# VectorE turns the later groups' tokens from reloaded rows, and ScalarE copies the diagonal squares of each state update: an attention and mixture-of-experts kernel on one Trainium2 core

## Chip, cores and metric

The kernel runs on one core of a Trainium2 chip (trn2), in one launch. The metric is the device time in microseconds (us). The engines are TensorE (PE), VectorE (DVE), ScalarE (ACT), GpSimd (POOL) and SyncE (SP), which issues most DMAs; they work side by side, each through its own instructions in order, and wait for one another on semaphores.

## What is computed

The input x has 4 x 1024 tokens of 512 features. Each token is normalised over its features (xn). Then comes chunked linear attention with 16 heads of 32 features and chunks of 128 tokens, cut here to what matters:

```python
q, k, v = silu(xn @ Wq), silu(xn @ Wk), silu(xn @ Wv)      # 16 heads of 32
for each chunk of 128 tokens:                             # S: 32 x 32 per head, starts at 0
    o = ((q k^T) * D) v + (q S) * q_decay
    S = chunk_decay * S + (k * k_decay)^T v
gate = (xn @ Wg1) @ Wg2
y = (rmsnorm per head of (o * sigmoid(gate))) @ Wo         # added to x
```

The second part is a mixture of 8 experts (512 to 2048 to 512, ReLU) over the same xn: each token goes to its two best experts by the logits xn @ Wg, an expert takes at most 1280, and the results, weighted by a softmax, are added to the output. The residual x is added too. All of it is float32; PE's products are made of three products of rounded high parts and remaining low parts (hi*hi, hi*lo, lo*hi).

## The kernel before

There are 32 tiles of 128 tokens. Attention works on groups of four tiles (512 tokens; `g` = 0 to 7, half a sequence each), and in each group on four units (`i` = 0 to 3, four heads each), 32 units `u` in all. After them come the experts, in which PE is busy without a gap; the change touches none of their code, except that some tensors lie elsewhere.

**Normalised tokens.** For each tile VectorE takes mean and variance (`norm_pair`, L971), GpSimd the power -0.5 (`norm_scale`, L549), VectorE writes `xn` (`normalise`, L982, the instruction L986). SP stores xn to DRAM (`store_xn`, L424), from where the experts gather it later. PE turns the tile with four 128x128 transposes into a PSUM bank (`turn_xn`, L1421, which calls `turn`, L1388, the instruction L1390). ScalarE copies the bank rounded to `xnT_hi` (`xnT_high`, L753), VectorE makes `xnT_lo`, the bank less the high part (`xnT_low`, L989). For group g + 1 this happens in unit i = 2 of group g, behind the last q projection of group g; tiles 2 and 3 of group g + 1 are normalised at the end of unit i = 1 of group g, tiles 0 and 1 at the end of the unit i = 3 before it (in group 0, all four in unit 0).

**Order on PE in a unit u** (L1580 to L1632): scores of u (`score`, L1427), state update of u (`update_states`, L1474, unless it was made ahead, as for i = 2 from group 1 on), gate of u (`project_gate`, L1470), k and q projections of u + 1 (`project`, L1396; 12 products of 128x512 each, listed under `product`, L1383), in unit i = 2 the transposes of xn, in unit i = 3 the small projection (L1407), then the transposes of the decayed k of u + 1 (`turn_kd`, L1465), attention of u (`attend`, L1489: products with the states L1502, with the masked scores L1508). In unit i = 1 the output projection of the group before follows (`project_out`, L1512), in unit i = 3 the v projection of the next group.

**Order on ScalarE in a unit** (L853 to L878): tanh of the gate, squares of the unit before, silu of k and of q of u + 1, in unit i = 2 the four high parts, then the copy of the turned k (`copy_kd`, L847), the high part of the attention output (`oT_high`, L804).

**Order on VectorE in a unit** (L1213 to L1273): the states, the masks on the four score banks (`mask`, L1014), the mean squares, scaling and turning back of earlier units, in unit i = 2 the four low parts, the gating (`gate_output`, L1091), a block transpose (`turn_gated`, L1096), in unit i = 1 residuals and the normalisation of two tiles.

**The state update.** PE writes kd^T v of each head into the diagonal 32x32 square of its chunk's 128x128 block in `t_bank`; the rest of the block holds old values. `states` (L1071) multiplies the bank by `same_head`, a 0/1 mask, into `update`, and then makes three steps of decay:

```python
step(v_.tensor_tensor(update[:, 0:n, :], by_chunk(t_bank[:, :])[:, 0:n, :],
                      same_head[:, :].unsqueeze(1).to_broadcast([P, n, P]), ALU.mult))
```

`n` is 4 in even groups and 3 in odd ones.

**SP's queue** is written out by hand (L448 to L526). At the start: the decays, four tiles of x, the four parts each of Wq and Wk, Wg1 and the router's Wg (one DMA each, into `small_raw`), Wg2 four times, the norm's weights, four stores of xn, then Wv and Wo (which wait for staging buffers), four more tiles of x. ScalarE reads `small_raw` behind the high parts of Wk, and the high parts of Wv after that.

## Time and profile before

| | us |
|---|---|
| median of 3 runs | 1984.32 (1983.89 to 1984.41) |
| the profiled execution | 1986.43 |
| its span, first to last instruction | 1984.7 |
| PE busy | 1972.2 (99%) |
| DVE busy | 906.7 (46%) |
| ACT busy | 552.5 (28%) |
| POOL busy | 730.1 (37%) |

The granted TensorE clock is 1.00 over the whole span (2.4 GHz). Shares of busy time are means over both parts of the kernel; the attention lies before some 535 us. Matmuls are pipelined: one of 128x512 shows as 0.39 us and the next starts 0.23 us after it, so a step's cost on PE is read from the starts of successive instructions. Times in a timeline are us from the start of the span; "x16" is the number of instructions merged in a row, and the brackets hold the idle time of the engine before it, with what ended it.

### The profile page before, as it was taken

What the parts mean: (1) busy time and instruction counts of PE and PEld (TensorE: products, weight loads), DVE (VectorE), ACT (ScalarE), POOL (GpSimd) and SP (SyncE); (2) the same over time, 40 slices, a digit from 0 to 9 for tenths busy, and PEclk for the clock granted to TensorE, in tenths of its full rate; (3) what the DMA queues carried; (4) which work ended last, traced back from release to release, by engine and by line L of the source; (5) the groups of instructions that cost most, each with busy time, mean ns of one, the idle gap of its engine ahead of it and who ended that gap; (6) DMA issues with size and microseconds to landing.
All of it is one profiled execution on the core that took longest, in us unless ns stands there. A gap on an engine that the chain in (4) does not pass through costs nothing.

```text
span 1984.7 us, 28995 instructions
## 1 busy us (share of the span) xinstructions
PE 1972.2 (99%) x11672; PEld 1631.0 (82%) x11672; DVE 906.7 (46%) x1839; ACT 552.5 (28%) x994; POOL 730.1 (37%) x608
## 2 busy tenths in 40 slices
PE   9999999999999999999999999999999999999998
PEld 7888888888888888888888888888888888888887
DVE  8777676777753234224323422432343234334311
ACT  6322232223332123124212312321242123123211
POOL 4645454545343324313342431333143324233321
PEclk9999999999999999999999999999999999999999
DMA  6112122211452134315233421522162125224121
GB/s 206 67 66 87 43 68 68 84 63 48 131 153 39 47 75 125 42 55 126 66 67 74 126 42 56 125 65 42 47 159 45 43 51 157 37 62 102 42 33 22
DMA packets 85638, 151.50 MB, mean 76 GB/s; under 512 B 18432, under 2 KB 18432, under 8 KB 85488
## 3 DMA queue, kind: packets, MB, share of 16 engines
q1 hardware_dynamic: 61312, 105.64, 16.8%
q0 software_dynamic: 24176, 43.76, 13.0%
q8 instruction: 106, 1.74, 0.4%
q14 instruction: 44, 0.36, 0.1%
HBM read 109.82 MB, written 39.53 MB: 75 GB/s over the span
## 4 chain that ended last, share of the span: by engine, by line
PE 97%; DVE 1%; SPq 1%; DMA 0%; issue 0%; POOL 0%; ACT 0%; DVEq 0%
PE bank L1383 47%; PE bank L1687 35%; PE bank L1519 5%; PE bank L1437 2%; PE bank L1508 2%; PE bank L1390 1%; PE bank L1502 1%; PE bank L1743 1%; PE bank L1730 1%; PE bank L1472 1%; PE bank L1411 1%; PE bank L1482 1%; DMA attn_raw<-in_L_attn_Wv 0%; PE bank L1531 0%; SPq L446 0%
## 5 line engine op out<-in xcount | busy, mean ns | idle before, releaser
L1303 DVE SCALAR_TENSOR_TENSOR h_lo<-bank,h_hi 128x512 fp32r<-128x512 f32 x254 | 175.3, 690 | 722.9 <-ACT h_hi L904 683.7
L682 POOL DMA_INDIRECT gathered<-xn_rows,gather_row x304 | 315.5, 1038 | 483.6 <-DVE x_blocks L1153 316.8
L1383 PE MATMUL bank<-xT_lo,w_hi 128*128 128x512 f32 x1024 | 398.5, 389 | 0.5 <-issue 0.5
L1383 PE MATMUL bank<-xT_hi,w_hi 128*128 128x512 f32 x1024 | 398.7, 389 | 0.0
L1383 PE MATMUL bank<-xT_hi,w_lo 128*128 128x512 f32 x1024 | 398.4, 389 | 0.0
L1687 PE MATMUL bank<-w_hi,h_hi 128*128 128x512 f32 x1016 | 395.2, 389 | 0.0
L1687 PE MATMUL bank<-w_lo,h_hi 128*128 128x512 f32 x1016 | 395.2, 389 | 0.0
L1687 PE MATMUL bank<-w_hi,h_lo 128*128 128x512 f32 x1016 | 395.2, 389 | 0.0
L904 ACT ACTIVATE h_hi<-bank 128x512 fp32r<-128x512 f32 x254 | 151.7, 597 | 795.5 <-PE bank L1383 756.3
L703 POOL DMA_INDIRECT out_rows<-y,add_row x64 | 103.9, 1624 | 435.7 <-ACT y L897 419.6
L1383 PEld LDWEIGHTS bank<-xT_lo,w_hi 128*128 128x128 f32 x1024 | 192.2, 188 | 40.9 <-issue 1.0
L1383 PEld LDWEIGHTS bank<-xT_hi,w_hi 128*128 128x128 f32 x1024 | 192.2, 188 | 40.8 <-issue 0.7
L1383 PEld LDWEIGHTS bank<-xT_hi,w_lo 128*128 128x128 f32 x1024 | 192.2, 188 | 39.9
L1687 PEld LDWEIGHTS bank<-w_lo,h_hi 128*128 128x128 f32 x1016 | 190.7, 188 | 39.8
L1687 PEld LDWEIGHTS bank<-w_hi,h_lo 128*128 128x128 f32 x1016 | 190.7, 188 | 39.6
L1687 PEld LDWEIGHTS bank<-w_hi,h_hi 128*128 128x128 f32 x1016 | 190.7, 188 | 39.4
L1123 DVE TENSOR_TENSOR w_lo<-raw_weights,w_hi 128x512 fp32r<-128x512 f32 x256 | 167.8, 684 | 84.8 <-ACT w_hi L802 64.9
L802 ACT CAST w_hi<-raw_weights 128x512 fp32r<-128x512 f32 x256 | 150.0, 618 | 98.3 <-DMA raw_weights<-in_L_ffn_w 78.8
L636 POOL TENSOR_TENSOR head_scale<-mean_sq,minus_half 128x16 f32<-128x16 f32 x32 | 104.4, 3264 | 20.7 <-DVE mean_sq L1025 20.2
L628 POOL DMA_INDIRECT slot_table<-record,slot_no x64 | 65.5, 1024 | 103.7 <-DVE slot_no L1069 47.4
L1018 DVE TENSOR_TENSOR scores<-bank,intra_decay 128x512 f32<-128x512 f32 x128 | 79.2, 681 | 0.4 <-PE bank L1437 0.3
L1163 DVE TENSOR_TENSOR xT_lo<-x_blocks,xT_hi 128x512 fp32r<-128x512 f32 x68 | 48.4, 711 | 52.3 <-ACT xT_hi L845 52.3
(225 smaller groups left out, 2298.5 us busy)
## 6 DMA issues: line engine op xcount, KB each, us to landing
raw_weights<-in_L_ffn_w SPq DMA_DIRECT2D x256, 256.0 KB
x_in<-in_L_attn_x SPq DMA_DIRECT2D x32, 256.0 KB, 4.0
xn_rows<-xn SPq DMA_DIRECT2D x32, 256.0 KB
x_res<-in_L_attn_x SPq DMA_DIRECT2D x32, 256.0 KB, 4.9
out_rows<-y_attn SPq DMA_DIRECT2D x28, 256.0 KB
gathered<-xn_rows,gather_row POOLq DMA_INDIRECT x304
out_rows<-y,add_row POOLq DMA_INDIRECT x88, 5.8
attn_raw<-in_L_attn_Wq SPq DMA_DIRECT2D x4, 256.0 KB, 4.7
```

The lines of the kernel that those rows point to most:

```text
L628: pool.indirect_dma_start(table[:, :], bass.IndirectOffsetOnAxis(ap=slot_no[:, t, i:i + 1], axis=0), record[:, t, i, :], None, bounds_chec ...
L636: g_.tensor_tensor(head_scale[:, u % 2, :], mean_sq[:, u % 2, :], minus_half[:, :], ALU.pow).then_inc(S["head_scale_ready"], 1)
L682: pool.indirect_dma_start(xg[:, nth % 2, q * P:(q + 1) * P], None, xn_pieces, bass.IndirectOffsetOnAxis(ap=gather_row[:, col, q:q + 1], ax ...
L703: pool.indirect_dma_start(out[:, :], bass.IndirectOffsetOnAxis(ap=add_row[:, col:col + 1], axis=0), y[:, i, :], None, compute_op=ALU.add). ...
L802: a.copy(unit_parts(u)[0], raw[:, u % UNITS, :]).then_inc(S["ffn_hi"], 1)
L904: a.activation(h_parts(e, j, f)[0][:, 0:n * P], h_bank[f % 2][:, 0:n * P], ACT.Relu).then_inc(S["h_hi_ready"], 1)
L1018: v_.tensor_tensor(by_chunk(scores[:, r, :]), by_chunk(sc[r][:, :]), decay_cols(intra_decay[:, u % GROUPS * HPG + r, :]), ALU.mult).then_i ...
L1123: v_.tensor_tensor(lo, raw[:, u % UNITS, :], hi.bitcast(F32), ALU.subtract).then_inc(S["ffn_lo"], 1)
L1303: v_.scalar_tensor_tensor(lo[:, 0:n * P], h_bank[f % 2][:, 0:n * P], 0.0, hi[:, 0:n * P].bitcast(F32), ALU.max, ALU.subtract).then_inc(S[" ...
L1383: last = mm(dest, at(left[l], t), at_r(right[r], t), start=(i == 0), stop=(i == n - 1))
L1519: last = mm(bank[:, :], oT[l][:, t, part], (w_hi["o"], w_lo["o"])[r][:, t, :], start=(start and t == ks[0] and l == r == 0), stop=(stop an ...
L1687: last = mm(y_bank[i][:, :], hx[:, part], wx[c][:, f % FPC, :], start=(f == 0 and l == 0), stop=(f == FT - 1 and l == 2))
```

## The change

1. The transposes of xn on PE fall away for groups 1 to 7. After its store, SP loads each tile of xn back from DRAM (`reload_pieces`), in four DMAs of 32 tokens each, 64 KB, 512 bytes per partition: 32-partition block q holds feature quarter q. VectorE turns the tile by one STREAM_TRANSPOSE of 128x512, which turns each 32x32 block by itself (`turn_pieces`): tiles 0 and 1 in unit i = 1, tiles 2 and 3 in unit i = 2. The high and low parts then read these blocks in SBUF. The result lies in the place of the tile before (`xn_blocks`), so `normalise` waits for low parts instead of transposes.
2. Features come into the k-tiles in another order, so the rows of Wq, Wk, Wv, Wg1 and the router's Wg are loaded in that order (`by_quad`), Wg1 and the router's Wg in four DMAs each instead of one. The first group's tiles are turned on PE by `turn_by_quads`, 16 products with 32 output partitions per tile.
3. In unit i = 3 PE's k projection takes the products by parts (`project_next_k`): hi*hi and lo*hi wait for the high parts, hi*lo for the low parts. The waits for low parts before the scores and the gate of that unit fall away. ScalarE's `copy_kd` stands between high parts 1 and 2.
4. ScalarE copies the four diagonal squares of the update (`copy_update`, four instructions of 32 partitions) into `update`, which is zeroed once; the multiplication and `same_head` fall away.
5. On VectorE the normalisation of tiles 2 and 3 moves ahead of residuals 2 and 3; SP's queue follows.

```diff
+            def reload_pieces(t):
+                j = t % TPG
+                sp.wait_ge(xn_stored[j], 16 * (t // TPG + 1))
+                for i in range(QUADS):
+                    first = t * P + i * HD
+                    sp.dma_start(xn[:, j, i * P:(i + 1) * P], xn_dram[first:first + HD, :].rearrange("s (q f) -> q s f", q=QUADS)
+                                 ).then_inc(xn_pieces_loaded[j], 16)
...
-            sp.dma_start(small_raw[:, :, 0:HD], wg1.rearrange("(t p) n -> p t n", p=P)).then_inc(S["small_loaded"], 16)
-            sp.dma_start(small_raw[:, :, HD:], w_route.rearrange("(t p) n -> p t n", p=P)).then_inc(S["small_loaded"], 16)
+            for t in range(DT):
+                sp.dma_start(small_raw[:, t, 0:HD], by_quad(wg1)[t]).then_inc(S["small_loaded"], 16)
+                sp.dma_start(small_raw[:, t, HD:], by_quad(w_route)[t]).then_inc(S["small_loaded"], 16)
...
                 if u == 0:
                     for t in range(TPG, 2 * TPG):
                         store_xn(t)
+                    for t in range(TPG, 2 * TPG):
+                        reload_pieces(t)
...
                 if i == 1 and g > 0:
-                    for j in range(TPG):
-                        store_y(TPG * (g - 1) + j)
+                    store_y(TPG * (g - 1))
+                    store_y(TPG * (g - 1) + 1)
                     if g < SUPERS - 1:
                         store_xn(TPG * (g + 1) + 2)
                         store_xn(TPG * (g + 1) + 3)
+                    store_y(TPG * (g - 1) + 2)
+                    if g < SUPERS - 1:
+                        reload_pieces(TPG * (g + 1) + 2)
+                        reload_pieces(TPG * (g + 1) + 3)
+                    store_y(TPG * (g - 1) + 3)
...
                     if g < SUPERS - 3:
                         load_x(TPG * (g + 3))
                         load_x(TPG * (g + 3) + 1)
+                    if g < SUPERS - 2:
+                        reload_pieces(TPG * (g + 2))
+                        reload_pieces(TPG * (g + 2) + 1)
...
+            def copy_update(u):
+                act.wait_ge(S["updated"], u + 1)
+                act.wait_ge(S["update_zeroed"], 1)
+                wait(act, ("attended", u))
+                n = carried_chunks(u)
+                for r in range(HPG):
+                    rows = slice(r * HD, (r + 1) * HD)
+                    last = a.copy(update[rows, 0:n, rows], by_chunk(t_bank[:, :])[rows, 0:n, rows])
+                last.then_inc(S["update_copied"], 1)
...
             for u in range(ATTN_UNITS):
                 g, i = u // GROUPS, u % GROUPS
+                copy_update(u)
                 act.wait_ge(S["gate_projected"], u + 1)
...
                 if i == 2 and g < SUPERS - 1:
                     for j in range(TPG):
+                        if j == 2:
+                            copy_kd(u + 1)
                         xnT_high(TPG * (g + 1) + j)
...
+            def turn_pieces(t):
+                j = t % TPG
+                dve.wait_ge(xn_pieces_loaded[j], 16 * QUADS * (t // TPG))
+                wait(dve, ("xn_turned", t))
+                v_.transpose(xn_blocks(j), xn[:, j, :]).then_inc(S["xn_turned"], 1)
...
-                dve.wait_ge(S["updated"], u + 1)
+                dve.wait_ge(S["update_copied"], u + 1)
                 dve.wait_ge(S["decay_made"], 1)
-                dve.wait_ge(S["consts_made"], 12)
-                step(v_.tensor_tensor(update[:, 0:n, :], by_chunk(t_bank[:, :])[:, 0:n, :],
-                                      same_head[:, :].unsqueeze(1).to_broadcast([P, n, P]), ALU.mult))
...
                 if i == 2 and g < SUPERS - 1:
+                    turn_pieces(TPG * (g + 1) + 2)
+                    turn_pieces(TPG * (g + 1) + 3)
                     for j in range(TPG):
                         xnT_low(TPG * (g + 1) + j)
...
+                if i == 1 and g < SUPERS - 1:
+                    turn_pieces(TPG * (g + 1))
+                    turn_pieces(TPG * (g + 1) + 1)
...
+            def turn_by_quads(bank, rows_of_tile):
+                for t in range(DT):
+                    for q in range(QUADS):
+                        rows, first = slice(q * HD, (q + 1) * HD), q * P + t * HD
+                        last = mm(bank[rows, t * P:(t + 1) * P], rows_of_tile[:, first:first + HD], ident[:, :], start=True, stop=True)
+                return last
...
+            def project_next_k(g):
+                pe.wait_ge(S["xnT_hi_made"], TPG * (g + 1))
+                for nth, (w_part, x_part, t) in enumerate(hi_hi + lo_hi + hi_lo):
+                    if nth == 2 * DT:
+                        pe.wait_ge(S["xnT_lo_made"], TPG * (g + 1))
+                    last = mm(proj[1][:, :], w_part["k"][:, t, 0:P], x_part[:, t, :], start=(nth == 0), stop=(nth == 3 * DT - 1))
+                last.then_inc(S["k_projected"], 1)
...
-                if i == 2 and g < SUPERS - 1:
-                    pe.wait_ge(S["masked"], HPG * (u + 1))
-                    turn_xn(g + 1, lambda j: pe.wait_ge(S["k_ready" if j == 2 else "q_ready"], u + 2) if j > 1 else None)
```

## Rows read from the trace of the kernel before

**Rows 1.** The page's chain of work that ended last, share by engine.
```profile
PE 97%; DVE 1%; SPq 1%; DMA 0%; issue 0%; POOL 0%; ACT 0%; DVEq 0%
```
**Rows 2.** PE's waits: line, released by, us in total, times, longest.
```profile
PE bank L1508 <- DVE scores L1018: 1.0, 1, 1.0
```
**Rows 3.** Timeline of PE at a group's turn: start us, us, what.
```profile
317.42 1.91 PE L1390 MATMUL bank<-ident,xn 128*128 128x128 f32 x16
319.16 0.60 PE L1390 MATMUL bank<-ident,kdT 128*128 128x128 f32 x4
...
322.48 0.46 PE L1482 MATMUL bank<-v,kd 128*32 128x32 f32 x32
...
323.20 0.39 PE L1383 MATMUL bank<-xnT_hi,wk_hi 128*128 128x512 f32 x1
323.43 0.40 PE L1383 MATMUL bank<-xnT_lo,wk_hi 128*128 128x512 f32 x1
```
**Rows 4.** Timeline of SP's queue in the start.
```profile
6.94 0.47 SPq L453 DMA_DIRECT2D small_raw<-in_L_attn_Wg  x1
7.46 0.54 SPq L454 DMA_DIRECT2D small_raw<-in_L_ffn_Wg  x1
...
12.84 2.78 SPq L446 DMA_DIRECT2D attn_raw<-in_L_attn_Wv  x4
```
**Rows 5.** Chain that ended last, the start: start us, us, what.
```profile
17.40 0.64 ACT wv_hi L767
...
37.89 1.44 DVE state L1083
...
42.15 1.08 PE bank L1508 x32
```
**Rows 6.** Timeline of VectorE, units i = 1 and i = 2 of a group.
```profile
302.46 0.69 DVE L1118 TENSOR_TENSOR y_attn<-bank,x_res 128x512 f32<-128x512 f32 x1 [1.70 <-PE bank L1519]
...
305.18 0.69 DVE L1118 TENSOR_TENSOR y_attn<-bank,x_res 128x512 f32<-128x512 f32 x1 [0.35 <-PE bank L1519]
...
311.23 0.99 DVE L986 TENSOR_SCALAR xn<-x_in,moments,rstd 128x512 f32<-128x512 f32 x2
312.13 0.68 DVE L1079 TENSOR_TENSOR update<-bank,same_head 128x512 f32<-128x512 f32 x1
...
317.80 0.71 DVE L1108 STREAM_TRANSPOSE normed<-squares 128x512 f32<-128x512 f32 x1
```
**Rows 7.** Issue to landing: x_in's 32 loads; slot_rec's eight, median.
```profile
DMA to landing us min/median/max: 3.1/4.0/6.5
...
slot_rec<-slot_table SPq DMA_DIRECT2D x8, 40.0 KB, 1.8
```
**Rows 8.** Timeline of PE: three tiles turned in quarters.
```profile
518.85 2.83 PE L1531 MATMUL bank<-ident,y 128*32 128x128 f32 x96
```
**Rows 9.** Timeline of ScalarE at the same turn as rows 3.
```profile
317.62 0.60 ACT L772 ACTIVATE qT<-bank 128x512 f32<-128x512 f32 x1 [2.12 <-PE bank L1383]
318.11 2.05 ACT L757 CAST xnT_hi<-bank 128x512 fp32r<-128x512 f32 x4
```
**Rows 10.** Groups by shape (busy us, mean ns); x_blocks' instructions (ns min/median/max).
```profile
L850 ACT COPY kd<-bank 128x384 f32<-128x384 f32 x16 | 7.8, 487 | 0.1
...
L845 ACT CAST xT_hi<-x_blocks x68: 619/622/625, 577.3 to 1887.5; 128x512 fp32r<-128x512 f32 x68
L1163 DVE TENSOR_TENSOR xT_lo<-x_blocks,xT_hi x68: 691/710/733, 578.0 to 1888.3; 128x512 fp32r<-128x512 f32 x68
```
**Rows 11.** Timelines of GpSimd and of VectorE, 317 to 355 us.
```profile
317.25 3.31 POOL L636 TENSOR_TENSOR head_scale<-mean_sq,minus_half 128x16 f32<-128x16 f32 x1 [0.39 <-DVE mean_sq L1025]
321.65 1.28 POOL L589 TENSOR_TENSOR qdT<-qT,q_decay 128x512 f32<-128x512 f32 x1 [1.09 <-PE bank L1508]
...
351.43 3.31 POOL L636 TENSOR_TENSOR head_scale<-mean_sq,minus_half 128x16 f32<-128x16 f32 x1 [0.80 <-DVE mean_sq L1025]
...
353.38 0.69 DVE L1112 TENSOR_TENSOR oT_lo<-normed,oT_hi 128x512 fp32r<-128x512 f32 x1 [0.68 <-ACT oT_hi L808]
```

More of the change, by code:

```diff
@@ L255, in build @@
         x_res_loaded = [sem(f"x_res_loaded{i}") for i in range(TPG)]
+        xn_pieces_loaded = [sem(f"xn_pieces_loaded{i}") for i in range(TPG)]
         xn_stored = [sem(f"xn_stored{i}") for i in range(TPG)]
@@ L380, in squares_of, with xn_blocks @@
             return squares[:, u % 2, :]
+        def xn_blocks(j):
+            return xn_first_blocks[:, :] if j == 0 else xn[:, j - 1, :]
         def turned_xn(t):
-            bank = (first_xn_bank if t < TPG else xn_bank)[t % TPG]
-            return bank[:, :].rearrange("p (t c) -> p t c", t=DT)
+            if t < TPG:
+                return first_xn_bank[t][:, :].rearrange("p (t q c) -> p t q c", t=DT, q=QUADS)
+            return xn_blocks(t % TPG).rearrange("p (q t c) -> p t q c", q=QUADS, t=DT)
         def small_bank(g):
@@ L415, in by_k_tile, with by_quad @@
             return blocks[:, :].rearrange("p (q t c) -> p t q c", q=QUADS, t=DT)
+        def by_quad(w):
+            return w.rearrange("(q t d) n -> t q d n", q=QUADS, t=DT)
         @block.sync
@@ L445, in load_weights @@
                 w = (wq, wk, wv, wo)[u // DT]
-                sp.dma_start(attn_raw[:, u % UNITS, :], w[u % DT * P:(u % DT + 1) * P, :]).then_inc(attn_raw_loaded[u % UNITS], 16)
+                rows = w[u % DT * P:(u % DT + 1) * P, :] if u // DT == WSET.index("o") else by_quad(w)[u % DT]
+                sp.dma_start(attn_raw[:, u % UNITS, :], rows).then_inc(attn_raw_loaded[u % UNITS], 16)
             sp.dma_start(ld_row[:, :], log_decay.partition_broadcast(P)).then_inc(S["decays_loaded"], 16)
@@ L755, in xnT_high @@
                 act.wait_ge(S["xn_turned"], t + 1)
-                wait(act, ("k_projected", GROUPS * (t // TPG)))
-                a.copy(xnT_hi[:, :, j * P:(j + 1) * P], turned_xn(t)).then_inc(S["xnT_hi_made"], 1)
+                wait(act, ("k_projected", GROUPS * (t // TPG)), ("q_projected", GROUPS * (t // TPG)))
+                a.copy(token_cols(xnT_hi, j), turned_xn(t)).then_inc(S["xnT_hi_made"], 1)
             def weights_high(n, ts=range(DT)):
@@ L864, in _ @@
                     for j in range(TPG):
+                        if j == 2:
+                            copy_kd(u + 1)
                         xnT_high(TPG * (g + 1) + j)
-                if i == GROUPS - 1 and g < SUPERS - 1:
-                    copy_logits(g + 1)
-                if u < ATTN_UNITS - 1:
+                elif u < ATTN_UNITS - 1:
+                    if i == GROUPS - 1:
+                        copy_logits(g + 1)
                     copy_kd(u + 1)
@@ L984, in normalise @@
                 dve.wait_ge(S["rstd_ready"], t // 2 + 1)
-                wait(dve, (xn_stored[j], 16 * (t // TPG)), ("xn_turned", t - TPG + 1))
+                in_use = ("xn_turned", t - TPG + 1) if t < 2 * TPG else ("xnT_lo_made", t - TPG + 1 + (j < TPG - 1))
+                wait(dve, (xn_stored[j], 16 * (t // TPG)), in_use)
                 v_.tensor_scalar(xn[:, j, :], x_in[:, j, :], moments[:, j, 0:1], rstd[:, j:j + 1],
@@ L990, in xnT_low @@
                 j = t % TPG
-                cols = slice(j * P, (j + 1) * P)
                 dve.wait_ge(S["xnT_hi_made"], t + 1)
-                v_.tensor_tensor(xnT_lo[:, :, cols], turned_xn(t), xnT_hi[:, :, cols].bitcast(F32), ALU.subtract).then_inc(S["xnT_lo_made"], 1)
+                v_.tensor_tensor(token_cols(xnT_lo, j), turned_xn(t), token_cols(xnT_hi, j).bitcast(F32),
+                                 ALU.subtract).then_inc(S["xnT_lo_made"], 1)
+            def turn_pieces(t):
[3 more added lines that the diff above has]
+                v_.transpose(xn_blocks(j), xn[:, j, :]).then_inc(S["xn_turned"], 1)
             def weights_low(n, ts=range(DT)):
@@ L1167, in _ @@
             v_.tensor_scalar(diff[:, :], diff[:, :], 0.0, None, ALU.max).then_inc(S["diff_ready"], 1)
+            v_.memset(update[:, :, :], 0.0).then_inc(S["update_zeroed"], 1)
             v_.memset(taken[:, :], 0.0).then_inc(S["carry_zero"], 1)
@@ L1257, in _ @@
                         normalise(TPG * (g + 1) + 3)
-                    else:
+                    add_residual(TPG * (g - 1) + 2, proj[0])
+                    add_residual(TPG * (g - 1) + 3, proj[1])
+                    if g == SUPERS - 1:
                         first_used = spares_of(dve, 0)
@@ L1430, in score @@
                 wait(pe, ("masked", HPG * u))
-                if u % GROUPS == GROUPS - 1 and u < ATTN_UNITS - 1:
-                    pe.wait_ge(S["xnT_lo_made"], TPG * (u // GROUPS + 1) + 2)
                 for c in range(TPG):
@@ L1527, in turn_first @@
                 pe.wait_ge(S["masked"], HPG * (ATTN_UNITS - 1) + sc.index(first_bank[i]) + 1)
-                for t in range(DT):
-                    for q in range(QUADS):
-                        rows, first = slice(q * HD, (q + 1) * HD), q * P + t * HD
-                        last = mm(first_bank[i][rows, t * P:(t + 1) * P], y[:, i, first:first + HD], ident[:, :], start=True, stop=True)
-                last.then_inc(S["x_turned"], 1)
+                turn_by_quads(first_bank[i], y[:, i, :]).then_inc(S["x_turned"], 1)
             pe.wait_ge(S["consts_made"], 6)
@@ L1540, in _ @@
             keep_clock(40)
[L1541 removed]
+            turn_first_xn()
             keep_clock(8)
```

41 lines of the change are left out of this document (16 added, 25 removed).

## The prediction

> **What bounds the kernel now.** I read the chain of waits first: TensorE (PE) holds 97% of the span [rows 1]. PE's own waits come next: after the start-up they come to 1.0 us for VectorE's masks, at the first attention product, and nothing else worth naming [rows 2]. So an instruction taken from PE after the start is worth its whole pitch, and any wait put in front of PE costs its whole length. Two places decide: the start (to 43 us), which hangs on DMA issues and VectorE, and the turn from one group of four tiles to the next, seven times.
>
> **Part 1: the transposes of xn leave PE.** In each of seven groups PE turns four tiles with 16 transposes, starting at 317.42 us; the next instruction, kd's transpose, starts at 319.16 [rows 3]. The pitch, not the 1.91 us busy, is the price: 1.74 us. 7 x 1.74 = **-12.2 us**. The four tiles of the first group stay on PE.
>
> **Part 2: the start.** SP issues serially, 0.47 and 0.54 us for the two small loads, and Wv's loads begin at 12.84 [rows 4]. The change makes these two loads eight: 8 x 0.47 - 1.0 = +2.75 us for all behind them. Wv's issue is on the chain: 4.56 us to its use by ScalarE at 17.40, from there VectorE's splits, routing and states, to the mask that PE awaits until 42.15 [rows 5]. ScalarE waits for the last small load in the same queue, so it shifts by the same 2.75. On VectorE the mask of unit 0 comes 2.75 later, less the 0.68 of the removed multiplication [rows 6]: +2.05. PE's own work after its count of choices, pushed by the same 2.75, reaches that product at 42.15 - 1.0 + 2.75 = 43.9, +1.75. The later one holds: **+2.0 us**. Bounds: if Wv lands in the shortest 3.1 us of [rows 7], 1.4 comes back, +0.6. If the eight reordered loads of Wq and Wk and the eight small ones all cost 0.54 instead of 0.47, it is 1.1 more, +3.1. One state update of this chain took 1.44 us [rows 5], long for its size; that may shrink (PE's own +1.75 then holds).
>
> PE turns the first tiles in quarters now. Three such tiles took 2.83 us [rows 8], 0.94 each against 0.44 by transposes. That is +2.0 us before 13 us, beside the queue's delay: the small loads and Wv come later still, so it costs nothing. Were the queue not late, it would be the bound, with some +1. The memset of `update` lies in VectorE's wait for its first load, and the two dropped affine selects free only GpSimd: nothing.
>
> **Part 3: the turn of the group, without the 1.74 us.** I take the group at 311 us as model, in its old times. PE's last q product ends where the transposes began, 317.42. The rest follows 1.74 earlier: the update starts at 320.74 instead of 322.48, the next k projection at 321.46 instead of 323.20 [rows 3]. That projection wants all four high parts at 321.46, all low parts after eight products of 0.23, at 323.3, and the q projection wants the tanh after twelve, at 324.2.
>
> ScalarE: silu q starts at 317.62, then high parts at a pitch of 0.51 [rows 9]. Read from SBUF such a cast takes 0.62 us [rows 10] instead of 0.61: nothing. Parts 0 and 1 end by 319.2, kd is copied by 319.8 (wanted at 320.7), parts 2 and 3 end by 320.9: **0.6 us to spare**.
>
> VectorE: residual 1 starts at 305.18; the two normalisations (0.99) move from 311.23 to behind it, into a wait for PE, and the multiplication (0.68) goes from 312.13. So turning back, which ended at 318.5, ends near 316.9 [rows 6]. Two block transposes of 0.71 (the same instruction and shape [rows 6]) end near 318.3. Each low part takes at most 0.71 [rows 10] and follows its high part; the last ends near 321.6 (wanted 323.3), the gating near 322.3. Tiles 0 and 1 are turned a unit earlier, 1.4 us for both in a 1.70 us wait for PE [rows 6]. Without that cover they would delay the first residual, after which PE still has a whole product row to do. Cost on the path: zero.
>
> ScalarE's copy of the diagonal squares is four instructions of 32x128. The nearest row is the 128x384 copy of 0.49 us [rows 10]; I take 0.25 each by length, 1.0 in all. Bounds: nothing, and 4 x 0.49 = 2.0. Behind PE's update, at 321.2, it ends at 322.2, so the tanh can run from 322.3 (the gating) to 322.9, with 1.3 us to spare; with 2.0 it still ends at 323.8, 0.4 to spare. Queued behind it are tanh, square and silu k. VectorE's states wait for the copy instead of multiplying, -0.68 + 1.0; PE waits for masks nowhere after the start [rows 2]. Zero.
>
> SP: per group 16 issues more, some 7 us of its time. The tight ones are tiles 2 and 3. Normalised by 306.9, stored from 306.5, a store lands after about 4.0 us, the median of x's loads of 256 KB [rows 7]. Eight issues of 0.47 follow, from 310.5 to 314.3; the last 64 KB land between 1.8 us (40 KB) and 4.0 us after their issue at 313.8 [rows 7]: 316 to 318. The last piece may land at 320.2 without a cost to PE (0.7 for the turn and 0.6 for the high part before 321.46). The store of y and the loads of x and residuals queued behind these issues are wanted tens of us later. Zero.
>
> **Sum.** -12.2 + 2.0 = -10.2. The profiled execution took 1986.43 us (span 1984.7 and 1.7 around it): it would give 1976.2. The runs' median is 1984.32, 2.1 lower: **1974.1 us**. Own range of this case: 0.6 to 3.1 at the start, 1972.7 to 1975.2.
>
> **A port against it.** What I see: VectorE's oT_lo, two SBUF inputs, started at 353.38 and took 0.69 us while GpSimd's head scaling ran from 351.43 to 354.74; the same scaling stands at 317.25 to 320.56 here [rows 11]. So I let the low parts run beside it, though they are new in having both inputs in SBUF (one was PSUM). The Trainium skill (SBUF — State Buffer, "Who interferes with whom") says that a VectorE operation with two SBUF inputs and a GpSimd one that reads SBUF exclude each other for the full instruction. By that rule the sum would be near zero (rival D); rows 11 speak against it for this scaling.
>
> **Rivals.**
> B, the start is cheap: what the issues delay had slack. Against: Wv's loads are in the chain itself. -12.2 with at most 0.6 back: 1972.1 to 1972.7.
> C, small waits: the 0.6 us of the high parts or the tanh's time are eaten by slower SBUF reads or GpSimd's decayed q (1.28 us [rows 11]) beside the low parts. For: three engines hand over in 4 us; against: each step above has its margin. 0.2 to 1.0 us x 7: 1975.5 to 1981.
> D, the port: low part 0 waits for 320.56, decayed q gets in between (1.3), low parts end at 324.4, the gating at 325.1, the tanh at 325.7 against 324.2: 1.5 x 7 = 10.5, 1984.6.
> E, slower than before: the reload comes late. Place: turning tile 3 of each group. With 6.5 us, the longest landing of [rows 7], for store and reload, and 0.54 per issue, the last piece lands at 306.5 + 6.5 + 7 x 0.54 + 6.5 = 323.3 instead of 320.2: 3.1 x 7 = 22, 1996. It decides the sign from 1.46 us per group (10.2 / 7), a landing after 321.7. Against: 6.5 is the longest of 32.
> F, PE spends the time otherwise (a lower granted clock or longer pitches): 1984. PE stays busy, so little for it.
>
> **Chances.** Forecast 0.56, B 0.10, C 0.21, D 0.05, E 0.06, F 0.02. A measurement tells 0.2% (4 us) from no change: faster is below 1980.4. Forecast, B and nearly all of C lie there: 0.85; same 0.08 (rest of C, D, F); slower 0.07 (E, a late D). The range takes B, the forecast and C, 1971.5 to 1980.5.
>
> **What would show it.** Right: PE has no transposes of xn after the start; kd's transpose follows the last q product at once in each third unit; the first attention product stands near 44.2 instead of 42.15; Wv is issued near 15.6. Wrong: PE idle ahead of the k projection released by ScalarE's xnT_hi (a late reload if VectorE waits for a DMA first; C otherwise), by VectorE's xnT_lo (D), or ahead of q by the tanh; or a first attention product at 42 to 43 us (B).

## The result and the profile after

The changed kernel is slower: 2012.62 us median of 4 runs (2010.08 to 2013.88) against 1984.16 us (1983.89 to 1984.41) for the kernel before on the same chip, a ratio of 1.0142 (95% interval 1.0127 to 1.0157). The forecast was 1974.1 (range 1971.5 to 1980.5) and faster. The profiled execution took 2011.84 us, its span is 2010.0. The profiled execution of the kernel before (1986.43) lies 2.3 us above its median, so the traces differ by 25.3 us where the runs differ by 28.5; where the 2.3 us lie is said further down.

**Where the time went.** Three starts of PE's products cut the attention into pieces. Timeline of PE of the changed kernel, at the first attention product and at the first product of the first and of the seventh output projection (columns as in [rows 3]):

```profile
74.91 1.08 PE L1562 MATMUL bank<-scores,v 128*32 128x128 f32 x32
...
138.81 0.50 PE L1573 MATMUL bank<-wo_hi,oT_hi 128*128 128x512 f32 x1
...
517.05 0.50 PE L1573 MATMUL bank<-wo_hi,oT_hi 128*128 128x512 f32 x1
```

The same two output projections of the kernel before:

```profile
106.13 0.50 PE L1519 MATMUL bank<-wo_hi,oT_hi 128*128 128x512 f32 x1
...
494.52 0.50 PE L1519 MATMUL bank<-wo_hi,oT_hi 128*128 128x512 f32 x1
```

| us | before | after | after less before |
|---|---|---|---|
| start to the first attention product | 42.15 | 74.91 | +32.8 |
| from there to the first output projection (holds the first turn of a group) | 63.98 | 63.90 | -0.1 |
| six more groups (six turns) | 388.39 | 378.24 | -10.2 |
| the rest, experts above all (span less the above) | 1490.2 | 1493.0 | +2.8 |
| span | 1984.7 | 2010.0 | +25.3 |

The turns of the groups pay (though 2.3 of the 10.2 us are not the change's doing, see under the table of experiments), and the start takes over three times as much back. PE's waits of the changed kernel say what the start waited for (columns as in [rows 2]):

```profile
PE bank L1432 <- DVE wv_lo L1051: 11.3, 4, 4.4
PE bank L1600 <- ACT xnT_hi L782: 5.8, 1, 5.8
PE bank L1600 <- ACT wk_hi L792: 3.8, 2, 1.9
PE bank L1588 <- POOL ident L578: 2.7, 1, 2.7
PE bank L1432 <- issue: 2.3, 1, 2.3
PE bank L1432 <- DVE g1T_parts L1059: 0.5, 1, 0.5
PE bank L1573 <- ACT tanh_g L894: 0.3, 1, 0.3
```

The first three, 20.9 us, are new but for 0.3 us, and all are high or low parts of loaded weights or of tokens queued behind them. The mask's wait of [rows 2] is gone. ScalarE's timeline shows the loads behind it, one 256 KB load per 2.67 us:

```profile
9.58 0.63 ACT L792 ACTIVATE wq_hi<-attn_raw 128x512 fp32r<-128x512 f32 x1 [2.42 <-DMA attn_raw<-in_L_attn_Wq]
12.25 0.63 ACT L792 ACTIVATE wq_hi<-attn_raw 128x512 fp32r<-128x512 f32 x1 [2.04 <-DMA attn_raw<-in_L_attn_Wq]
...
22.94 0.63 ACT L792 ACTIVATE wk_hi<-attn_raw 128x512 fp32r<-128x512 f32 x1 [2.04 <-DMA attn_raw<-in_L_attn_Wk]
```

And SP's queue, which answers to [rows 4]:

```profile
3.13 2.45 SPq L467 DMA_DIRECT2D attn_raw<-in_L_attn_Wq  x4
5.62 11.03 SPq L467 DMA_DIRECT2D attn_raw<-in_L_attn_Wk  x4
16.69 2.55 SPq L475 DMA_DIRECT2D small_raw<-in_L_attn_Wg  x1
...
34.17 3.33 SPq L467 DMA_DIRECT2D attn_raw<-in_L_attn_Wv  x4
```

Wq's four issues still take 0.6 us each. Wk's four and the first three small ones take about as long as a load, 2.55 to 3.2 us: SP stands in its queue, which I read as full. The small loads wait there, and Wv is issued at 34.17 instead of 12.84 [rows 4]. The table of windows says how much moved (first a window, then busy us and number of instructions of each engine, granted PE clock, share of the 16 DMA engines, GB/s); after:

```profile
10.00:20.00 10.00, 4.46 (x136) 4.02 (x124) 2.27 (x5) 3.88 (x8) 1.18 (x7) 0.91 0.27 100
20.00:30.00 10.00, 5.95 (x12) 3.57 (x13) 4.30 (x8) 2.67 (x5) 0.00 (x0) 0.50 0.25 80
```

and before, 10 to 20 us:

```profile
10.00:20.00 10.00, 9.71 (x51) 7.79 (x51) 9.92 (x18) 9.43 (x24) 1.53 (x10) 1.00 1.09 358
```

With everything waiting for weights, the DMA engines were a quarter busy. That is as much as 4 of 16 at full work, each moving its part at its usual rate (358 / 16 is 22 GB/s, 100 / 4 is 25). PE, left idle, then ran its few products at a granted clock of 0.50, the 1.2 GHz level.

### The profile page after: what moved, and what is told of

The parts are those of the page before. It is cut to its first block, busy times and chain, and to the rows that moved or that the text cites. A ratio compares the mean times of both kernels' runs of the same rounds, so it can differ in the third digit from the quotient of the medians.

```text
span 2010.0 us, 29268 instructions
## 1 busy us (share of the span) xinstructions
PE 1976.5 (98%) x11672; PEld 1625.5 (81%) x11672; DVE 920.1 (46%) x1836; ACT 584.6 (29%) x1122; POOL 732.4 (36%) x606
## 4 chain that ended last, share of the span: by engine, by line
PE 94%; SPq 2%; DMA 2%; DVE 1%; issue 1%; ACT 0%; POOL 0%; DVEq 0%; ACTq 0%
PE bank L1432 46%; PE bank L1745 35%; PE bank L1573 4%; PE bank L1491 1%; PE bank L1562 1%; PE bank L1801 1%; PE bank L1788 1%; PE bank L1556 1%; DMA attn_raw<-in_L_attn_Wv 1%; PE bank L1439 1%; SPq L467 1%; DMA xn<-xn_rows 1%; PE bank L1460 1%; PE bank L1615 1%; PE bank L1526 1%
## 5 line engine op out<-in xcount | busy, mean ns | idle before, releaser
L1166 DVE TENSOR_TENSOR w_lo<-raw_weights,w_hi 128x512 fp32r<-128x512 f32 x256 | 167.7, 685 | 83.5 <-ACT w_hi L827 83.2
```

The lines of the kernel that those rows point to most:

```text
L1166: v_.tensor_tensor(lo, raw[:, u % UNITS, :], hi.bitcast(F32), ALU.subtract).then_inc(S["ffn_lo"], 1)
```

## The experiments

The medians of the kernel before on the chips used lie between 1984.16 and 1987.62 us, so a time counts only beside the kernel before of its own chip. "Start" is the time of the first attention product, "groups" the six intervals between output projections.

| kernel | us (before there) | ratio, 95% | start | groups |
|---|---|---|---|---|
| before | 1984.16 | | 42.15 | 388.39 |
| after | 2012.62 (1984.16) | 1.0142, 1.0127 to 1.0157 | 74.91 | 378.24 |
| b_split4 | 1986.67 (1986.68) | one run | 42.45 | 388.44 |
| b_small8 | 1989.37 (1986.68) | one run | 45.87 | 388.40 |
| a_stride4 | 1984.21 (1986.68) | one run | 46.33 | 380.57 |
| a_all | 1978.87 (1986.68) | 0.9960, 0.9946 to 0.9975 | 43.68 | 378.25 |
| a_q32 | 1987.72 (1984.36) | one run | 51.39 | 379.26 |
| b_dims | 2008.63 (1984.36) | one run | 66.07 | 386.14 |
| a_quarter | 2009.14 (1984.36) | one run | 75.46 | 376.11 |
| a_all48 | 1974.24 (1984.36) | 0.9949, 0.9933 to 0.9966 | 43.26 | 376.12 |
| a_all40 | 1977.69 (1984.43) | 0.9963, 0.9952 to 0.9975 | 43.22 | 376.15 |
| b_keep48 | 1990.37 (1984.43) | 1.0030, 1.0019 to 1.0042 | 43.69 | 386.14 |
| a_mult | 1982.22 (1984.43) | 0.9988, 0.9978 to 0.9997 | 44.71 | 381.91 |
| b_copy | 1983.07 (1984.43) | 0.9995, 0.9985 to 1.0005 | 40.93 | 386.14 |
| b_quad | 2014.84 (1987.62) | 1.0136, 1.0119 to 1.0153 | 69.52 | 388.48 |
| a_keep48 | 2011.21 (1987.62) | 1.0119, 1.0102 to 1.0136 | 73.71 | 381.76 |

In seven traces (before, b_split4, b_small8, a_stride4, a_all, b_quad, a_keep48) the seventh output projection comes late, by 2.1 to 2.4 us where a like group is there to compare, behind stops of PE without a releaser. a_all shows them, and the identical a_all40 on another chip does not. The six of them that are experiments are all those of two chips, on which the kernel before has its two highest medians (1986.68 and 1987.62); none of the eight traces of the two other chips (medians 1984.36 and 1984.43) shows them. So this much of a "groups" figure goes with the chip or the hour and not with the kernel.

### Is it the pattern of the weight loads?

**b_split4**, the kernel before with the rows of its loads split 4 x 32, though they follow one another in memory:

```diff
-sp.dma_start(attn_raw[:, u % UNITS, :], w[u % DT * P:(u % DT + 1) * P, :])
+rows = w[u % DT * P:(u % DT + 1) * P, :].rearrange("(q d) n -> q d n", q=QUADS)
+sp.dma_start(attn_raw[:, u % UNITS, :], rows)
```

> The kernel before, where the loads of Wq, Wk and Wv keep their natural rows and only their access pattern is written as 4 x 32 rows instead of 128. Theory S (spread: a load whose DRAM pattern begins with a dimension of 4 is served by 4 of the core's 16 DMA engines, so that 256 KB take the 2.67 us seen between the changed kernel's high parts of Wq, and the queue behind them stands): the same 2.67 us between Wq's high parts, the DMA share near 0.26 in that stretch, the first attention product (L1508, at 42.15 in the kernel before) at 58 to 68 us, the whole at 2000 to 2010. Rival R (rows scattered in DRAM make the reordered loads slow): nothing changes, 42 us and 1984. Rival N (the number of small loads, 8 instead of 2, does it): also 42 us and 1984.

Nothing changed (start 42.45). Such a split describes the same unbroken run of rows, so it tests nothing about scattered ones. A test needs a pattern whose pieces don't follow one another.

**b_small8**, the kernel before with its two small loads as eight, of consecutive rows:

```diff
-sp.dma_start(small_raw[:, :, 0:HD], wg1.rearrange("(t p) n -> p t n", p=P))
-sp.dma_start(small_raw[:, :, HD:], w_route.rearrange("(t p) n -> p t n", p=P))
+for t in range(DT):
+    sp.dma_start(small_raw[:, t, 0:HD], wg1[t * P:(t + 1) * P, :])
+    sp.dma_start(small_raw[:, t, HD:], w_route[t * P:(t + 1) * P, :])
```

> The kernel before, where only the two small loads (Wg1 and the router's Wg) are made as eight, each of 128 natural rows. My prediction's term: Wv's issue 2.75 us later, the first attention product at 44.2 us instead of 42.15 and the whole +2.0 us, 1986. Theory S says the same, since each of these loads begins with 128 rows. Rival N (the count of small loads is what costs the changed kernel its start): first attention product beyond 60 us, 2004 or more.

The start came 3.4 us after b_split4's and the run took 2.7 us more (one run of each). This is the part of the start that the prediction had priced (+2.0, bounds 0.6 to 3.1), somewhat above it.

**a_stride4**, the changed kernel with every fourth feature in one k-tile: a load then takes every fourth row, one per partition, and its pattern begins with 128. VectorE writes xn in the matching order.

```diff
-return w.rearrange("(q t d) n -> t q d n", q=QUADS, t=DT)
+return w.rearrange("(p t) n -> t p n", t=DT)
...
-v_.tensor_scalar(xn[:, j, :], x_in[:, j, :], moments
+v_.tensor_scalar(xn[:, j, :].rearrange("p (q t f) -> p q f t", q=QUADS, t=DT),
+                 x_in[:, j, :].rearrange("p (q f t) -> p q f t", q=QUADS, t=DT), moments
```

> The changed kernel with another order of features: xn is written with every fourth feature of a quarter together, so that k-tile t holds rows t, t+4, t+8 ... of each weight, and each load of Wq, Wk, Wv (and of the experts' first matrix) has one dimension of 128 rows with a stride of four rows. The eight small loads stay eight. Theory S: high parts of Wq follow each other at ScalarE's own pace (0.67 us), first attention product at 44 to 45 us instead of 75.0, the whole at 1976 to 1979 (before - 12.2 + 2.0 + 2 for waits at the groups' turns). Rival R (scattered rows): the rows are more scattered than in the changed kernel, so 75 us and 2010 stay.

28.6 of the 32.8 us were back, with rows that are scattered more than the change's. The forecast was missed all the same: a start of 46.33 where 44 to 45 was expected, and 1984.21 us where 1976 to 1979 was. Of the excess, some 2 us are the stops before the seventh projection and 2.4 another stop (further down). The edit also gives the experts' first matrix this order. That is not what brings the time back: behind the seventh output projection, a_keep48 with the old pattern takes 1489.5 us and a_all48 with the new one 1489.1. **a_all** adds to it two small loads instead of eight and the reload of a_quarter (below):

> As the kernel with every fourth feature together, and besides: the small loads are two again, and the four reloads of a tile go by quarters of features (32 partitions x 4 x 512 bytes, first dimension 32) instead of by 32 tokens (first dimension 4). Theory S: each reload is spread over 16 DMA engines, tile 3 no longer makes VectorE wait at the group's turn, first attention product at 42 to 43 us, the whole 1971 to 1974, about 0.6% below the kernel before. If the waits at the turn come from GpSimd beside the low parts instead (rival D of the prediction, in small), they stay, and it is 1973 to 1976.

It gained, though less than forecast (1978.87 for 1971 to 1974, start 43.68 for 42 to 43). Its remaining loss led to the questions further down.

**a_q32** keeps every row of the changed kernel in its slot and turns only the loads round: one takes the 128 rows of a feature quarter, 32 partitions by 4 slots.

```diff
-sp.dma_start(attn_raw[:, u % UNITS, :], by_quad(w)[u % DT])
+sp.dma_start(attn_raw[q * HD:(q + 1) * HD, base:base + DT, :],
+             w[q * P:(q + 1) * P, :].rearrange("(t d) n -> d t n", t=DT))
```

> The changed kernel with the same weight rows in the same slots, fetched the other way round: one load takes the 128 features of a quarter (32 partitions, 4 slots each, so the pattern begins with 32) instead of 4 quarters of one slot (the pattern begins with 4); the gating and routing weights likewise. Bytes, addresses, order and number of loads are the same. Theory S (a load whose pattern begins with a dimension of 4 runs on 4 of the 16 DMA engines): Wk's last load lands by 28 us, Wv is issued by 18 us, the first attention product comes at 44 to 48 us and the span is 1979 to 1985 us. Rival R (2 KB rows from scattered places are slow by themselves): the loads still come one per 2.7 us, first attention product at 70 to 76, span about 2010.

23.5 us came back and rival R fell: the same rows in as many loads don't come one per 2.7 us. But the start missed its forecast of 44 to 48, and Wv was issued at 19.42, not by 18. Two things in the trace may be why; they were not priced apart: the first high part now needs all four loads of its weight (it starts at 12.36, in the changed kernel at 9.58), and the DMA engines were fully busy yet moved 210 GB/s, where the kernel before moved 358. Window of a_q32:

```profile
10.00:20.00 10.00, 7.86 (x146) 5.90 (x141) 6.04 (x11) 6.31 (x12) 1.17 (x7) 1.00 1.12 210
```

**b_dims** makes a scale of it: the kernel before with the first dimension 2 for Wq, 8 for Wk, 16 for Wv.

```diff
+n = (2, 8, 16, 1)[u // DT]
+rows = w.rearrange("(q t d) n -> t q d n", q=n, t=DT)[u % DT]
```

> The kernel before, with the rows of Wq, Wk and Wv taken in other orders, so that their loads begin with a dimension of 2, 8 and 16 (it leaves the order of the features against the tokens wrong, so attention's values differ; the work is the same). Theory S (16 engines divided by the first dimension): Wq's four loads come one per 5.3 us, Wk's one per 1.3 us, Wv's at the full rate, 0.7 us or less each. Rival R (scattered rows are slow whatever the pattern's first dimension): Wq, Wk and Wv come at one and the same spacing, near 2.7 us. Rival W (each load's reordering is free, the queue's depth was the trouble): all under 1 us.

Timeline of ScalarE, where Wq (2) and Wk (8) arrive:

```profile
11.84 0.63 ACT L769 ACTIVATE wq_hi<-attn_raw 128x512 fp32r<-128x512 f32 x1 [4.73 <-DMA attn_raw<-in_L_attn_Wq]
17.19 0.63 ACT L769 ACTIVATE wq_hi<-attn_raw 128x512 fp32r<-128x512 f32 x1 [4.72 <-DMA attn_raw<-in_L_attn_Wq]
...
33.01 0.63 ACT L769 ACTIVATE wk_hi<-attn_raw 128x512 fp32r<-128x512 f32 x1 [0.59 <-DMA attn_raw<-in_L_attn_Wk]
34.35 0.63 ACT L769 ACTIVATE wk_hi<-attn_raw 128x512 fp32r<-128x512 f32 x1 [0.71 <-DMA attn_raw<-in_L_attn_Wk]
```

and its window from 15 to 20 us, when only Wq's loads ran:

```profile
15.00:20.00 5.00, 0.00 (x0) 0.00 (x0) 0.00 (x0) 0.63 (x1) 0.00 (x0) 0.50 0.14 50
```

5.35 us per load with 2, 2.67 with 4, 1.34 with 8: inverse to the first dimension, at 0.14 and 0.26 of the engines for 2 and 4. The figure for 8 is one pair of starts. Wv's spacing (16) is hidden by other waits and was not read off.

**b_quad** puts the change's own pattern, alone, into the kernel before.

```diff
+rows = w.rearrange("(q t d) n -> t q d n", q=QUADS, t=DT)[u % DT]
```

> The kernel before with one thing of the change: Wq, Wk and Wv are loaded by the changed kernel's pattern, one row block of each of the 4 quarters (it leaves the order of the features against the tokens wrong, so attention's values differ; the work is the same). Theory S: the pattern that begins with 4 costs the start by itself: one Wq or Wk load per 2.67 us, first attention product at 70 to 74 us instead of 42, time 28 to 33 us above the kernel before, 2012 to 2017. Rival: most of the changed kernel's loss needs its eight small loads or its turns by quarter as well, and this alone costs under 20 us.

Start 69.52, ratio 1.0136 against the change's 1.0142. So the pattern of Wq, Wk and Wv by itself is 27.4 of the 32.8 us. The start ended just under the expected band; the time is inside 2012 to 2017, but only 27.2 us above the kernel before of its chip, for 28 to 33. The other 5.4 us of the start come with what the changed kernel adds. In its trace eight small loads stand in the slow queue (Wv issued at 34.17 there, 29.49 here); this part was not tested by itself.

The Trainium skill ("DMA: Bandwidth & Descriptors", "How many engines (k)") states the rule: the number of engines is the largest up to 16 that divides the slowest dimension of both patterns. The runs agree at 2, 4 and 8. By that rule alone the eight loads of Wq and Wk would have been priced at four times their time. So they would by the trace of the kernel before, as the last part shows.

### What a turn of a group is worth

**a_quarter**, the changed kernel with its reload turned round: 32 source rows per partition block come first, instead of the 4 feature quarters.

```diff
-sp.dma_start(xn[:, j, i * P:(i + 1) * P], xn_dram[first:first + HD, :].rearrange("s (q f) -> q s f", q=QUADS))
+sp.dma_start(by_chunk(xn[i * HD:(i + 1) * HD, j, :]),
+             xn_dram[t * P:(t + 1) * P, i * P:(i + 1) * P].rearrange("(c s) f -> s c f", c=QUADS))
```

> The changed kernel, the reload of the normalised rows alone turned round (32 rows of each of the 4 row blocks, pattern beginning with 32, instead of 32 rows by 4 stretches of 512 bytes, also beginning with 32 in the source). Theory: the start is untouched (first attention product 74 to 76), the turning of tile 3 waits less for its reload than the 0.7 us of the changed kernel, span 2008 to 2011. Rival: the reload matters more than its waits show, and the span falls under 2006.

(The text on record says that the changed kernel's reload also begins with 32. It doesn't, it begins with 4 and is the same fault in small.) VectorE's waits of the changed kernel had this line:

```profile
DVE xn L1040 <- DMA xn<-xn_rows: 6.9, 6, 1.6
```

In a_quarter it is gone and the six groups take 376.11 instead of 378.24 us. While the pieces of tile 3 are under way (401 to 404 us in both traces) the DMA share is 0.25 in the changed kernel and 0.48 in a_quarter. So 0.35 us a group was rival E in small: VectorE turned tile 3 late and passed it on. In the changed kernel, VectorE at a turn:

```profile
410.06 0.71 DVE L1040 STREAM_TRANSPOSE xn<-xn 128x512 f32<-128x512 f32 x1 [0.69 <-DMA xn<-xn_rows]
410.70 0.65 DVE L1032 TENSOR_TENSOR xnT_lo<-xn_first_blocks,xnT_hi 128x512 fp32r<-128x512 f32 x1
411.27 2.97 DVE L1032 TENSOR_TENSOR xnT_lo<-xn,xnT_hi 128x512 fp32r<-128x512 f32 x3
414.16 0.67 DVE L1137 SCALAR_TENSOR_TENSOR gated<-tanh_g,bank 128x512 f32<-128x512 f32 x1
```

and GpSimd beside it:

```profile
407.44 3.39 POOL L661 TENSOR_TENSOR head_scale<-mean_sq,minus_half 128x16 f32<-128x16 f32 x1
410.92 1.57 POOL L614 TENSOR_TENSOR qdT<-qT,q_decay 128x512 f32<-128x512 f32 x1
```

**b_copy**, the kernel before with the second half of the change alone (ScalarE's four copies, no multiplication):

> The kernel before with that half alone: ScalarE copies the diagonal squares, VectorE no longer multiplies, TensorE still turns the tokens. Theory: neither engine bounds the units here, so the time stays that of the kernel before within 1.5 us. Rival: the copies (0.96 us before each unit's tanh) delay the gate, TensorE waits for it in each unit, and the time rises by 0.2 to 0.5 us a unit, 6 to 15 us in all; or, the other way, the states come earlier and the kernel gains 1.5 to 4 us.

Within 0.1% of the kernel before. The groups keep their old pace, 64.56 and 64.15 us in turn. The start is 1.2 us earlier and PE's wait for the mask is gone. **a_mult**, the reverse: a_all48 (below) with the multiplication back on VectorE.

```diff
-copy_update(u)
...
+step(v_.tensor_tensor(update[:, 0:n, :], by_chunk(t_bank[:, :])[:, 0:n, :],
+                      same_head[:, :].unsqueeze(1).to_broadcast([P, n, P]), ALU.mult))
```

> a_all48 with VectorE's multiplication by the same-head table in place of ScalarE's four copies (both tables built as in the kernel before). It prices the second half of the change. Theory P (the copies are what keeps VectorE in time at the turn of a group): VectorE carries 0.62 us more in each of 31 units, the low parts of the turned tokens come later, TensorE waits at the turn, and the time is 2 to 6 us above a_all48's, 1976 to 1980. Rival Q (VectorE has room; the copies only move work): within 1 us of a_all48's 1974.2 (ratio to before 0.994 to 0.9955).

Theory P held, and more than expected: 8 us above a_all48, for 2 to 6. 5.8 of them are in the groups, 1.5 in the start and 1.5 between the start and the first output projection; the experts were 0.4 faster. PE's waits name VectorE, at another place than expected, the gate's low part of the next group:

```profile
PE bank L1442 <- DVE g1T_parts L1065: 4.0, 7, 0.9
```

The two halves belong together: the copies alone bring nothing that the runs can tell, and without them most of what the turns save goes back into VectorE's waits.

### A stop of PE that comes and goes with eight instructions far ahead of it

The changed kernel has a stop that the kernel before doesn't have, in the third expert, with no releaser. In the program it stands two products behind the branch over the code of the spare blocks, which lies in the middle of each expert. Timeline of PE, after:

```profile
1009.08 0.39 PE L1432 MATMUL bank<-xT_lo,w_hi 128*128 128x512 f32 x1
1011.75 0.80 PE L1432 MATMUL bank<-xT_hi,w_lo 128*128 128x512 f32 x1 [2.28 <-issue]
1012.34 0.63 PE L1432 MATMUL bank<-xT_hi,w_hi 128*128 128x512 f32 x1
1012.77 0.63 PE L1432 MATMUL bank<-xT_lo,w_hi 128*128 128x512 f32 x1
```

It stands in front of the same product in a_stride4, a_all, a_q32 and a_quarter (2.28 to 2.51 us). Here and in a_all PE comes back at the lower clock: the next products follow at 0.43 us instead of 0.23. The kernel before has 0.54 us at the like place of its seventh expert (the texts on record say the eighth, and count the two halves of an expert as experts of their own in places):

```profile
1718.86 0.50 PE L1383 MATMUL bank<-xT_lo,w_hi 128*128 128x512 f32 x1 [0.54 <-issue]
```

**a_all48** is a_all with eight transposes more at the start, where PE waits for x anyway:

```diff
-keep_clock(40)
+keep_clock(48)
```

> a_all with 48 instead of 40 transposes that keep TensorE's clock up at the start, while it waits for x; nothing else in the program is other, but TensorE's later instructions lie 8 places further on. Theory I (the 2.5 us stop two products into an expert, without a releaser, is TensorE running out of fetched instructions at one place of its code): the stop goes or moves to another product; if it goes, the time falls by 3 to 4.5 us to 1974.5 to 1976. Rival J (the stop belongs to the work, its data or its timing): it stays at the second product of an expert with 2.3 to 2.5 us and the time is a_all's 1978.9.

> a_all once more (40 transposes at the start), to stand beside its pair with 48 on one chip's kernel before. Theory I (TensorE's stop of 2.5 us belongs to the place of its code): the stop is there again at the third product of the same expert, and the ratio to the kernel before is 0.9965 to 0.998, 2 to 3 thousandths above that with 48 (0.9949). Theory J (the stop comes and goes by chance): no stop, and a ratio near 0.995.

> The kernel before with 48 instead of 40 transposes at the start, while TensorE waits for x. The kernel before has a stop of 0.54 us without a releaser at the second product of its eighth expert. Theory I: eight instructions more move the places of the code, so this stop changes its size or its expert, and the time moves by up to 3 us either way while the work up to there keeps its times. Theory J: the stop stays at 0.2 to 0.8 us in the eighth expert and the time is that of the kernel before within 1 us.

> The changed kernel with 48 transposes at the start instead of 40. Theory I (TensorE's stop of 2.28 us in the third expert belongs to the place of its code): as in the pair of a_all, the stop is gone, and the time falls 2 to 4 us to 2008.5 to 2010.5; ratio to before 1.012 to 1.013. Rival J: the stop stays.

The stop did what theory I said in all four; the sizes were at or beyond the edge of what was expected (a_all48 1974.24 for 1974.5 to 1976, a_all40 0.9963 for 0.9965 to 0.998, a_keep48 2011.21 for 2008.5 to 2010.5, b_keep48 5.9 us for up to 3). With 48, a_all and the changed kernel lose the stop altogether, and a_mult, with 48 too, has none; a_all40, on a third chip, has it again at the same product (2.21 us). The pair gives 0.9949 against 0.9963, of which the intervals overlap, so the size of the gain, some 2 to 3 us, rests on the traces. The changed kernel with 48 has a ratio of 1.0119 against 1.0142, again with overlapping intervals. In the kernel before the same eight instructions do the opposite. A stop of 1.56 us appears in the second expert and that in the seventh grows from 0.54 to this, with the low clock behind it:

```profile
1720.51 0.80 PE L1383 MATMUL bank<-xT_hi,w_lo 128*128 128x512 f32 x1 [2.45 <-issue]
1721.11 0.63 PE L1383 MATMUL bank<-xT_hi,w_hi 128*128 128x512 f32 x1
1721.53 0.63 PE L1383 MATMUL bank<-xT_lo,w_hi 128*128 128x512 f32 x1
```

It is 6 us slower for it, interval clear of 1. All six traces of the changed kernel's family with 40 have the large stop in the third expert, although they reach it at times from 978 to 1012 us, and none of the three with 48 has. That speaks for the place of PE's code and against its timing, but no run moved the code without adding instructions, and the mechanism was not tried. The small stop of the kernel before has another size in each trace (0.16 us in b_small8, 0.82 in b_split4) though PE's code is the same there.

## Why the prediction was wrong

**What bounds the kernel, right.** PE was the bound, and a wait put in front of it cost its whole length: PE's three new waits make up 20.9 of the 32.8 us of the start. The rest was not divided further; the lower clock between 20 and 60 us (granted 0.50, 0.74, 0.60 and 0.55 in steps of 10 us) is a part of it.

**Part 1, right in size, one turn short.** In six groups the change saved 10.2 us against 6 x 1.74 = 10.4. That near match is luck, of two things that cancel: 2.3 us of the old 388.39 are the stops that go with the chip, and 2.1 us was lost to the late reload. Cleaned of both, a group went from 64.36 us (half of 64.57 + 64.14) to 62.66 (a_quarter, a_all48, half of 62.83 + 62.49): 1.70 against 1.74. The seventh turn, the one in group 0, gave 0.1 instead of 1.74, also in a_all48 (63.90). There VectorE still carries work of the start. In a_all48 PE's k projection at 65 to 68 us runs 0.6 us long and the gate's low part costs 0.5 more at 79 us.

**Part 2, the step that failed.** "SP issues serially, 0.47 and 0.54 us": the eight reordered loads of Wq and Wk, and Wv's, were priced by their issues alone, with at most 1.1 us for a slightly longer issue. The term that was missing is the transfer. A load whose pattern begins with the 4 quarters runs on a quarter of the DMA engines, 2.67 us instead of about 0.7. Wq and Wk are then 21 us of transfer, and once some of them are under way each issue behind them takes as long. The diff's `rearrange("(q t d) n -> t q d n")` was where to see it, and its price stood in the trace of the kernel before, which loads the experts' first matrix by that very pattern (`unit_source`, L372). SP's timeline there, and the window in which four such loads of 256 KB run almost alone (columns as in the windows above):

```profile
448.06 7.54 SPq L468 DMA_DIRECT2D raw_weights<-in_L_ffn_w  x8
...
508.76 2.47 SPq L468 DMA_DIRECT2D raw_weights<-in_L_ffn_w  x4
```

```profile
512.00:522.00 10.00, 9.90 (x211) 8.32 (x210) 8.77 (x18) 6.05 (x12) 6.47 (x3) 1.00 0.28 101
```

That is 101 GB/s, 2.6 us a load, against 358 GB/s in the start (window of 10 to 20 us above). Even the slow issue is there: of the eight in a row from 448.06 the sixth took 2.64 us. In the experts ScalarE waits for such loads (83.5 us in all) and PE doesn't, so they cost nothing; in the start PE waits too. The small loads' own term, +2.0, measured 3.4 by itself. "The longest landing" of rival E looked at the reload with the same blind spot; it cost 0.35 us a group, where the rival had 3.1.

**The turns by quarters, right.** They cost nothing while the queue was late. Where the queue is not (a_all48) the start is 43.26, with PE busy throughout from 10 us: the "+1" that the prediction gave for this case.

**Part 3, right, with thinner margins.** ScalarE's copies took 0.95 to 1.07 us for four (1.0 forecast). The block transposes took 0.67 to 0.71. The low parts did not take "at most 0.71" each: at every turn one of the later three took 1.67 to 1.78 us, and the three together 2.97 in the turn shown.

**The rivals.** B is out. C and E came as a small mix: 2.1 us in six groups, by the reload. D was half right: head scaling (3.39 us) held nothing up, but GpSimd's decayed q did, for 1.1 us per turn, and that fitted into the margin. The reason for a slower kernel, which had 7 in 100, was none of those named. The fault was one of listing: each edit was costed on the queue that issues it, and none on the engines that move it.

**With the start mended** the forecast's range would have held: a_all40 took 1977.69 us beside 1984.43, and a_all48 1974.24 beside 1984.36, 0.5% faster than the kernel before. That the latter meets 1974.1 so closely is partly luck. The turn of group 0 is missing from its gain (1.6 us), the start cost 1.1 instead of 2.0, and the rest of the kernel is 1.1 us shorter (half of that is the stop of 0.54 us, gone here), which the prediction didn't have.

## What to carry to other kernels

When an edit reorders what a DMA reads, write down the outermost dimension of its pattern whose pieces don't follow one another in memory: here 2, 4 and 8 gave an eighth, a quarter and a half of the full pace, and behind a few slow loads the issues became slow as well. Then look whether the old kernel already has such a load somewhere, even where it costs nothing: its pace can be read there. Look for it as a low DMA share in a stretch where engines wait for DMAs. Bring such dimensions to the inside, by 32 partitions first or, better, by a feature order that gives each partition its own row. And where PE stops without a releaser, shift its code by a few instructions, and compare kernels on one chip, before explaining the difference by the edit.

## What the runs showed of the hardware that was not expected

- The time of a 256 KB load goes inversely with the first dimension of its pattern: 5.35 us at 2, 2.67 at 4, 1.34 at 8 (one pair). Behind several such loads SP issues at the same pace: 2.55 us an issue instead of 0.43 to 0.54.
- Loads of the same bytes into 32 partitions by 4 slots kept the DMA engines busy (share 1.12) but moved 210 GB/s, against 358 into 128 partitions.
- VectorE and GpSimd hold each other up in some pairs only. Beside the decayed q (128x512, two SBUF inputs) a low part took 1.78 us, otherwise 0.68; beside head scaling (128x16, 3.4 us) the low parts kept their time (22 of the attention output's, 0.69 us each). The 1.44 us of the state in [rows 5] is the same: the decayed k of GpSimd ran from 37.86 to 39.15. In b_copy, where they don't meet, that instruction takes 0.35. The Trainium skill ("SBUF — State Buffer", "Who interferes with whom") gives the exclusion as a rule for every such pair; the traces agree for the decayed q and k and not for the scaling.
- Eight more instructions on PE, which cost little where they stand, came with a time 6 us longer in one kernel and stops of 2.2 to 2.5 us gone in two others (by the traces; the intervals of the times overlap there).
- Stops of PE of some 2 us in all, ahead of the seventh output projection, stand in all six traces of two chips and in none of the eight of two others, whatever the kernel.
